# Key columns and inverse sums transposed into two banks and split in halves, with the class strips ahead and the chunk means moved into the pairs' loop

## The reference

```python
AC = jnp.einsum('bqhd,bkhd->bhqk', q + u, k)
BD = jnp.einsum('bqhd,khd->bhqk', q + v, kr)
prob = jax.nn.softmax((AC + BD) * inv_sqrt_d, axis=-1)
vec = jnp.einsum('bhqk,bkhd->bqhd', prob, val).reshape(b, s_len, H * DH)
h = layer_norm(h + vec @ W_o[i], ln1_g[i], ln1_b[i])
```

## Time and profile before

| | |
|---|---|
| median of 3 runs | 2613.9 us (2610.91 to 2614.98) |
| the profiled execution | 2615.31 us |
| its span, first to last instruction | 2613.5 us |
| PE busy | 2233.3 us (85%) |
| DVE busy | 1846.4 us (71%) |
| ACT busy | 1614.7 us (62%) |
| POOL busy | 1187.9 us (45%) |
| mean granted clock of PE | 0.973 of full speed |
| chain that ended last | PE 34%, ACT 31%, DVE 11%, issue 7%, POOL 5%, SP 4% |

### The profile page before, as it was taken

One profiled execution on the slowest core, in us unless ns is written; L12 is line 12 of the kernel. 1 busy time (PEld: TensorE's weight loads), 2 busy tenths in 40 slices (PEclk: granted clock), 3 DMA queues, 4 the chain that ended last, 5 costly groups with the idle time before them and its releaser, 6 DMA issues.

```text
span 2613.5 us, 61377 instructions
## 1 busy us (share of the span) xinstructions
PE 2233.3 (85%) x19254; PEld 1641.1 (63%) x19254; DVE 1846.4 (71%) x5687; ACT 1614.7 (62%) x5077; POOL 1187.9 (45%) x2205
## 2 busy tenths in 40 slices
PE   0259999999989999999989999999899999987998
PEld 0136666666766666667656666667666666665565
DVE  8837777777767777777757777777678777776533
ACT  2126667767666677776656667766676766665322
POOL 3025555555456555554544555554565555541211
PEclk9679999999999999999999999999999999998999
DMA  4344444435554343444644444445543343355110
GB/s 162 88 136 112 113 103 105 105 99 145 143 157 119 99 102 102 103 122 132 183 117 115 105 104 104 104 139 143 157 100 91 86 102 90 94 144 178 50 45 22
DMA packets 378062, 295.38 MB, mean 113 GB/s; under 512 B 45087, under 2 KB 350721, under 8 KB 376739
## 3 DMA queue, kind: packets, MB, share of 16 engines
q1 hardware_dynamic: 370603, 272.41, 39.9%
q10 hardware_dynamic: 4864, 12.68, 1.4%
q0 software_dynamic: 2272, 6.35, 0.7%
HBM read 137.71 MB, written 72.07 MB: 80 GB/s over the span
## 4 chain that ended last, share of the span: by engine, by line
PE 34%; ACT 31%; DVE 11%; issue 7%; POOL 5%; SPq 4%; DMA 1%; ACTq 0%; POOLq 0%; DVEq 0%
ACT e_rows L2144 12%; PE bk L2024 6%; PE bk L1898 6%; PE bk L2059 4%; PE bk L1273 4%; ACT pt L2129 4%; SPq L1532 3%; ACT pt L2204 3%; ACT rel L2079 3%; ACT rel L2203 2%; DVE pt L2445 2%; PE bk L2048 2%; POOL arena L1726 2%; PE bk L1886 2%; PE bk L1854 2%
## 5 line engine op out<-in xcount | busy, mean ns | idle before, releaser
L2144 ACT ACTIVATE e_rows<-e_rows,nb 128x257 f32<-128x257 f32 x1024 | 518.0, 519 | 40.8 <-DVE nb L2334 39.9
L2334 DVE CUSTOM_DVE_ANT_0 e_rows<-bk,arena 128x257 f32<-128x257 f32 x1024 | 390.0, 418 | 72.6 <-PE bk L1931 71.4
L1838 PE MATMUL bk<-hin,arena 128*128 128x257 f16 x3072 | 424.0, 275 | 10.2 <-ACT rel L2079 6.6
L2296 DVE TENSOR_TENSOR pt<-bk,pt 128x512 f16<-128x512 f32 x512 | 353.8, 691 | 77.2 <-ACT pt L2129 70.1
L1886 PE MATMUL bk<-ident,e_rows 128*128 128x128 f32 x2048 | 325.0, 281 | 70.7 <-ACT e_rows L2144 52.4
L1724 POOL TENSOR_SCALAR arena<-rel 128x257 f16<-128x257 f32 x496 | 202.6, 409 | 356.2 <-ACT rel L2079 352.0
L1726 POOL TENSOR_TENSOR arena<-rel,arena 128x257 f16<-128x257 f32 x496 | 327.4, 660 | 41.3
L1838 PEld LDWEIGHTS bk<-hin,arena 128*128 128x128 f16 x3072 | 298.1, 98 | 61.2 <-issue 9.2
L1886 PEld LDWEIGHTS bk<-ident,e_rows 128*128 128x128 f32 x2048 | 221.2, 141 | 159.3 <-ACT e_rows L2144 131.4
L2129 ACT ACTIVATE pt<-bk 128x512 f16<-128x512 f32 x512 | 311.6, 609 | 8.1 <-PE bk L1886 8.0
L1774 POOL TENSOR_SCALAR wf<-wf 128x256 f32<-128x256 f32 x216 | 93.0, 431 | 424.6 <-DMA wf<-in_w_dram 254.1
(11 more groups left out here) (328 smaller groups left out, 4278.6 us busy)
## 6 DMA issues: line engine op xcount, KB each, us to landing
arena<-arena SPq DMA_DIRECT2D x768, 128.5 KB
wf<-in_w_dram SPq DMA_DIRECT2D x168, 128.0 KB, 2.9
w_split_dram<-wh SPq DMA_DIRECT2D x168, 128.0 KB, 2.2
xs_dram<-in_c_blank_dram SPq DMA_DIRECT2D x24, 772.5 KB
wf<-in_we_dram SPq DMA_DIRECT2D x96, 128.0 KB, 2.7
we_split_dram<-wh SPq DMA_DIRECT2D x96, 128.0 KB, 1.8
w_rest<-w_split_dram SPq DMA_DIRECT2D x12, 1024.0 KB, 17.0
arena<-we_split_dram SPq DMA_DIRECT2D x8, 1536.0 KB, 11.5
```

Source lines behind the costliest of these rows:

```text
L1838: r_ = mm(bank[4 + s % 2][:, 0:S], wcol(a, C_QKV, k, 3 * HD, chunk_at(s)), hin[:, m, k, :], start=i == 0, stop=i == 5)
L2144: act.activation(E[:, h % 2, qt, :], E[:, h % 2, qt, :], ACT.Exp, bias=nb[:, 2 * h + qt:2 * h + qt + 1], scale=-1.0, accum_out=sums[:, qt, ...
L2296: v.tensor_tensor(pt[:, h, 1, :, 0:IMG], bank[2 + h % 2][:, :].rearrange("p (k s) -> p k s", k=QT), pt[:, h, 0, :, 0:IMG], ALU.subtract).t ...
L2334: v.tensor_tensor_reduce(E[:, h % 2, qt, :], bank[qt][:, 0:S], cb[:, h, :], -SCORE, 3e38, ALU.add, ALU.min, nb[:, 2 * h + qt:2 * h + qt + ...
```

## The change

- PE transposes the inverse sums first, into bank 4, and signals; then the class key columns, into bank 6, and signals again. In both banks the result lies in the left half.
- ACT does the class strip first, behind a wait for `ecr` instead of one for the transposes. Then it copies each half of 256 columns as its pair of transposes comes, the inverse sums (t = 1) first.
- DVE makes the strip of `pkr`, then the half of the inverse sums, then that of the class key.
- PE's first replication waits for the strip and the first half only. Ahead of the first product it waits for the second half and for `vbd`, which it waited for ahead of the replication so far.
- DVE's two chunk means ahead of the loop move into it, behind the `o_part` calls of rounds c = 2 and c = 4.

```diff
-                for i, src in enumerate((ecol, rs)):
+                for src, out in ((rs, bank[4]), (ecol, bank[6])):
                     for qt in range(QT):
-                        r_ = pe.transpose(bank[6][:, (i * QT + qt) * P:(i * QT + qt + 1) * P], src[:, qt, :], ident[:, :])
-                r_.then_inc(key_done, 1)
+                        r_ = pe.transpose(out[:, qt * P:(qt + 1) * P], src[:, qt, :], ident[:, :])
+                    r_.then_inc(key_done, 1)
...
-                        pe.wait_ge(key_lo, at(2, 2))
-                        pe.wait_ge(vbd_in, at(64, 64))
+                        pe.wait_ge(key_lo, at(3, 2))
                     if c >= 2:
                         pe.wait_ge(rb_ok, at(8, c - 1))
                     mm(bank[RB[c % 2]][:, 0:S], sel[:, c, :], pkr[:, 1, :], start=True, stop=True).then_inc(rb_done, 1)
+                    if c == 0:
+                        pe.wait_ge(key_lo, at(3, 3))
+                        pe.wait_ge(vbd_in, at(64, 64))
                     mm(bank[OB[c % 3]][:, 0:S], vbd[:, c * P:(c + 1) * P], pkr[:, 0, :], start=False, stop=True).then_inc(o_done, 1)
...
-                act.wait_ge(key_done, at(1, 1))
-                act.activation(pkh[:, :, 0:IMG], bank[6][:, :].rearrange("p (t s) -> p t s", t=2), ACT.Copy).then_inc(key_hi, 1)
+                act.wait_ge(rs_ok, at(6, 6))
                 act.activation(pkh[:, :, CLS:S], ecr[:, :, :], ACT.Copy).then_inc(key_hi, 1)
+                for i, t in enumerate((1, 0)):
+                    act.wait_ge(key_done, at(2, i + 1))
+                    act.activation(pkh[:, t, 0:IMG], bank[(6, 4)[t]][:, 0:IMG], ACT.Copy).then_inc(key_hi, 1)
...
-                v.wait_ge(key_hi, at(2, 2))
-                v.scalar_tensor_tensor(pkr[:, :, 0:IMG], pkh[:, :, 0:IMG], lo_row[:, 0:1], bank[6][:, :].rearrange("p (t s) -> p t s", t=2),
-                                       ALU.mult, ALU.add).then_inc(key_lo, 1)
+                v.wait_ge(key_hi, at(3, 1))
                 v.scalar_tensor_tensor(pkr[:, :, CLS:S], pkh[:, :, CLS:S], lo_row[:, 0:1], ecr[:, :, :], ALU.mult, ALU.add).then_inc(key_lo, 1)
+                for i, t in enumerate((1, 0)):
+                    v.wait_ge(key_hi, at(3, i + 2))
+                    v.scalar_tensor_tensor(pkr[:, t, 0:IMG], pkh[:, t, 0:IMG], lo_row[:, 0:1], bank[(6, 4)[t]][:, 0:IMG],
+                                           ALU.mult, ALU.add).then_inc(key_lo, 1)
...
-                if kind is MIDDLE or kind is CLOSING:
-                    chunk_mean(at, l, kind, 0, 0)
-                    chunk_mean(at, l, kind, 1, 1)
...
+                    if c in (2, 4) and (kind is MIDDLE or kind is CLOSING):
+                        chunk_mean(at, l, kind, c // 2 - 1, c // 2 - 1)
```

More of the change, by code:

```diff
@@ L2375, in body @@
                         v.wait_ge(e_ok, at(32, 24))
-                        v.wait_ge(key_done, at(1, 0))
+                        v.wait_ge(key_done, at(2, 0))
                         for j in range(3):
```

## The result

| | before | after |
|---|---|---|
| median (lowest to highest of 5 runs) | 2613.9 us (2606.87 to 2617.78) | 2602.59 us (2600.13 to 2603.3) |
| ratio after to before, 95% interval | | 0.9963 (0.9949 to 0.9977) |
| profiled execution, its span | 2615.31, 2613.5 us | 2603.3, 2601.5 us |
| mean granted clock of PE | 0.973 | 0.978 |

A forecast was written before the change was run, and what follows sets the result against it. PE was taken to wait 1.7 us an iteration on a serial ACT-DVE relay. 0.92 + 21 x (0.99 - 0.1) + 3 x 0.5 + 7 x 0.55 = 25.0, 34 with the clock, gave 2580 us, range 2571 to 2597.

The forecast's parts named there:

- (a) to (e): PE-ACT-DVE relay behind the key transposes: pv(3) at 2.75 instead of 3.74; gain 0.99 us in 21 iterations, opening 0.92.
- (c): Class strips first on ACT and DVE: hidden in both; 0.2 us an iteration if DVE's cover were gone.
- (f): Two chunk means inside the loop: pv(6) taken as 0.1 us late an iteration; 1.2 if fully exposed.
- the loop gives it back: Means hold DVE before multiplies, delaying PE's wait ahead of pv(c+2): 23 of 34 us gone, 2603; chance 0.08.
- (g): Three layer entries: line 2009 instead of line 2008 waits for vbd; gain 0.5 us each, bounds 0 and 0.6.
- (h): Seven routing iterations: line 2008 starts near 1.82 instead of 2.37, behind the residual's matmuls; gain 0.55 us each.
- (i): PE's clock: all six 1.2 GHz stretches behind PE's gaps go; gain 9 us, bounds 0 and 10.
- the clock falls as before, or elsewhere: PE's gaps don't vanish and the falls' phase is chance: gain only 25 us, 2589; chance 0.22.
- the halves don't overlap: DVE's first half waits for ACT's second, line 2008 starts 0.3 us later: 2587; chance 0.08.
- it doesn't do what it says: PE's waits are bound by something the trace names wrongly, relay stays at 3.74: 2614 us; chance 0.02.
- slower: The loop's spread-out first matmuls bring the clock down in every iteration: price 39 us, 2628; chance 0.02.

The follow-up runs named there:

- no_means: The changed kernel without any chunk mean, so POOL splits the plain weights and part of the computation is left out; 2586.42 us, ratio 0.9893.
- pool_behind_loop: The changed kernel, both means in the loop, but POOL waits for the last o_part before its chunks of middle and closing iterations; 2582.91 us.
- both_means_behind: The changed kernel with both chunk means behind the pairs' loop, ahead of sum_squares; 2586.85 us, ratio 0.9904.
- one_mean_in_loop: The changed kernel with the first mean kept in the loop behind pair 2 and the second moved behind the loop; 2584.34 us, ratio 0.9893.
- rows_ahead: The changed kernel with first mean ahead of the loop, second behind it, plus routing rows loaded ahead of the second stack of copies; 2576.19 us.
- means_in_loop_only: The kernel before with only the two chunk means moved into the loop; 2624.29 us, ratio 1.0046.
- strips_first_only: The kernel before with only the class strips put ahead of the 512-column instructions on ACT and DVE; 2602.82 us, ratio 0.9962.

## Why the prediction was wrong

**(a) to (e), the relay: right.** Four starts were forecast for the middle iterations and hit within 0.01 to 0.02. A half takes 0.48 on DVE and 0.38 on ACT, and the strip on DVE lies at T + 0.56. One bound of (c) was met where I saw none: in the opening, in the three entries and in iteration 26 the strip takes 0.70 instead of 0.22, and in the first four of these line 2007 is 0.27 late. Timeline of the opening after (T is 216.03):

```profile
216.59 0.70 DVE L2391 SCALAR_TENSOR_TENSOR pkr<-pkh,lo_row,ecr 128x2 f16<-128x2 f16 x1
216.60 0.67 POOL L1782 TENSOR_TENSOR wh<-wf,wh 128x256 f16<-128x256 f32 x1
...
217.74 0.28 PE L2007 MATMUL bk<-pkr,sel 128*128 128x257 f16 x1 [0.27 <-DVE pkr L2394]
```

It is POOL again, beside an instruction of two elements. So the opening gained 0.55 and not 0.92. In no_means this happens in 22 of the 32 iterations, and line 2007 starts at 1.70 there (but at 1.83 in iteration 26).

**(f), the means in the loop: this step failed.** I priced a mean at the multiply behind it and at pv(6), 0.1 an iteration, with 1.2 as the end of the scale. pv(6) isn't late at all: it starts 3.34 behind pv(3). The price is paid at the end of the loop, and it is 1.0 in 19 of the 21 iterations, 0.5 in one and nothing in one, some 20 us, which is what pool_behind_loop gave back (19.7). Two things were left out. I looked only at who waits for the multiply, the nearest consumer, while PE's output projection waits for the last `o_part`; behind the second mean the loop can make up little: undisturbed (both_means_behind) the multiplies lie 1.12 apart and the last two 0.89, and 0.89 is what DVE needs for a pair, so that 0.2 is slack ahead of the seventh multiply and nothing ahead of the eighth. And of the second part of (f), the chunks that POOL makes later, I asked whether they would be too late, not what they would lie beside. In the kernel before the same collisions lay behind the first pairs, where the loop makes them up; the longest `o_part` of 925 ns beside a median of 420, in the group of line 2305 above, was there to be read.

**The rival "the loop gives it back"** named the right part and came out at the measured 2603, but by another mechanism: it put the loss at pv(c + 2) and took the means' own 1.2 us for it. Both are refuted, the place by pv(6), the size by one_mean_in_loop (0.1 for a mean alone) and pool_behind_loop (nothing for both). Its sum fitted by accident.

**(g), entries.** 0.5 each was forecast, 2.0 each was measured in this pair of profiles, and 2.0 of the 6.0 is what iteration 8 lost. The relay of the kernel after is as described, but the transfer's own time is not the same from profile to profile: the multiply of an entry starts on average at 3.3 after T in the kernel after and at 3.4 to 5.0 in its eight variants, all with the same relay, and at 4.6 to 5.7 in the four profiles with the relay of before or only its strips moved. The means of the two groups are 4.1 and 5.2, so that my estimate of the gain is 1.2 an entry, more than was forecast; why more isn't shown.

**(h), routing.** Line 2007 moved as forecast, the gain of 3.9 did not arrive: the rows' transfer, issued by SP at its own time, ends last. Rows 4 end with the multiply; I should have followed the gain past the output projection to line 253, whose waits of 2 to 5 us stand in the profile of before too. rows_ahead shows that this was the next wait.

**(i), the clock.** 9 us were taken for six falls in one profile. A second profile of the same kernel has two, so the medians that are compared hold fewer than six. The 46 runs of the kernel before that stand beside the variants give a size: their mean granted clock is 0.9751, that of the five runs after 0.9778, and among the 46 a run is 1.9 us shorter for each 0.001 that its clock is higher. That makes 5 us, an estimate. Falls there are, and their price of 1.5 was right; the step that fails is to take one profile's six for all runs. The profiles of after and of its eight variants have none behind the gaps of these 21 iterations. That speaks for the shorter gaps as the cause, but means_in_loop_only and strips_first_only have none either, with gaps of 0.92 and 0.70 and of 0.70 and 0.76, and their 19 runs have a granted clock of 0.976 to 0.979. So a gap of that length is not enough for a fall, and what brings one about stays open. Nor did I count that a fall can turn up elsewhere: iteration 8 of the kernel after has one at line 1863, and the iteration is 2.0 us longer; iteration 16 has one too.

The rivals "the clock falls as before, or elsewhere", "the halves don't overlap", "it doesn't do what it says" and "slower" didn't come true, by the same rows: no fall behind the gaps in the 21, line 2007 at 1.44, pv(3) at 2.76. Of the first only "elsewhere" is true in part, at the ends of iterations 8 and 16.

With (f) at 1.0 instead of 0.1, (g) at the entries' 6.0 less iteration 8's 2.0, (h) at 0.1 in all and (i) at 5, the sum is 0.55 + 21 x 0 + 4.0 + 0.1 + 5 = 9.7; 11.3 was found. pool_behind_loop, the change as the forecast understood it, is at 2582.9, within the forecast's own range of 2573 to 2586. That is luck in part: the middle iterations are as forecast there, but the 3.9 of (h) are missing in it as well, and (g) and (i) came out at other sizes.

Still open: in iterations 27 to 31 of most variants ACT waits 0.5 longer for the first replication than in the kernel after (1.57 against 1.01), with line 2007 at the same time. I found no cause, and it hides part of what these variants gain in the routing iterations. That POOL's work can be late without cost is shown for this kernel only up to the delays tried here.

## What to carry to other kernels

Follow a gain to the last consumer of the stage, not to the first wait that it shortens; the two places where it was lost lay some 9 and 12 us behind the first multiply. When an instruction is moved, look up whom it releases and beside what the released work will then run, the more so for GpSimd's work on SBUF tiles beside VectorE's. Take a clock fall that one profile shows as chance until a second profile shows it at the same place, and look at the granted clock of all runs before a gain is put down to the edit: strips_first_only is 9 us faster with iterations of nearly the old length.

## What the runs showed of the hardware that was not expected

VectorE and GpSimd hold each other up, and the profile shows it as a longer instruction, not as idle time. Beside GpSimd's TENSOR_SCALAR of 0.48 an `o_part` (two inputs in SBUF, 128x257) took 0.67 instead of 0.42, beside its TENSOR_TENSOR of 0.67 it took 0.84; a two-element SCALAR_TENSOR_TENSOR from SBUF took 0.70 instead of 0.22. The end fits a full stop: `o_part` ends 0.27 to 0.29 after GpSimd's instruction, the two-element one 0.02 after it (217.27 and 217.29). The multiply, one of whose inputs is in PSUM, isn't touched: 66 multiplies of the kernel after start while a GpSimd instruction runs, and they take 0.41 to 0.43 as the others do. GpSimd can be the one that waits, as in iteration 10 (0.77 instead of 0.48), and in three routing iterations its TENSOR_TENSOR, recorded 0.07 or 0.08 behind an `o_part`, takes 0.87 or 0.88 instead of 0.67 while the `o_part` keeps its 0.42. The Trainium skill, page "SBUF — State Buffer", section "Who interferes with whom", has the rule: a VectorE instruction with two inputs in SBUF and a GpSimd instruction that reads SBUF share a read interface, and whoever comes second waits for the whole instruction, while a VectorE instruction with at most one input in SBUF, outside its two-port modes, isn't touched. The trace agrees, by the numbers above, but for the order: at 216.59 VectorE's strip is recorded 0.01 ahead of GpSimd's instruction and is still the one that waits, and at 839.93 GpSimd's is recorded 0.08 ahead of the `o_part` and waits, so that the records don't settle who came first. GpSimd's spans in a profile are rough; VectorE's longer instructions and the 19.7 us of pool_behind_loop don't rest on them. With that rule in hand, step (f) could have been priced beforehand.
